# Attention of a two-layer vision block: the engines' loop over 364 window pairs replaced by straight code

## What is computed

```python
qkv = jnp.einsum('bhwc,cd->bhwd', x, w_qkv)
qkv = qkv + jnp.concatenate([q_bias, jnp.zeros_like(q_bias), v_bias])
qkv = jnp.roll(qkv, (-SHIFT, -SHIFT), axis=(1, 2))
...
q = _l2norm(q) * jnp.exp(scale)
k = _l2norm(k)
attn = jnp.einsum('bnhqd,bnhkd->bnhqk', q, k)
...
attn = attn + bias + jnp.asarray(_SHIFT_MASK)
attn = jax.nn.softmax(attn, axis=-1)
out = jnp.einsum('bnhqk,bnhkd->bnhqd', attn, v)
...
return jnp.einsum('bhwc,cd->bhwd', out, w_proj) + b_proj
```

## Time and profile before

| | us |
|---|---|
| median of 3 runs | 10940.03 |
| lowest and highest | 10927.17, 10954.37 |
| the profiled execution, its own time | 10950.05 |
| its span in the trace | 10948.2 |
| busy: GpSimd | 6207.5 (57%) |
| busy: VectorE | 5565.9 (51%) |
| busy: TensorE | 4602.7 (42%) |
| busy: ScalarE | 3954.9 (36%) |

### The profile page before, as it was taken

The page is one execution under the profiler, slowest core; times in us unless marked ns, Lnnn a source line. Parts: engine busy times, 40 slices in busy tenths (PEclk is TensorE's granted clock), DMA queues, the critical chain, the costliest instruction groups (busy, mean ns, idle before and its releaser), DMA issues. The chain is left out here.

```text
span 10948.2 us, 130025 instructions
## 1 busy us (share of the span) xinstructions
PE 4602.7 (42%) x31813; PEld 2736.9 (25%) x31813; DVE 5565.9 (51%) x14498; ACT 3954.9 (36%) x9657; POOL 6207.5 (57%) x6259
## 2 busy tenths in 40 slices
PE   0011777777775998874232222322323323223000
PEld 0011555555553544551111111111101101101000
DVE  9987999999996776551211211212212112112477
ACT  0011877777782554332121211212212212112255
POOL 0000545444451222666777777777777777777675
PEclk9755999999897999876666666666666666666555
DMA  0000111111112222553222222222222222222366
GB/s 21 0 0 36 38 34 37 37 38 37 37 34 85 62 61 75 145 136 60 45 49 44 45 48 44 47 45 46 47 44 47 48 41 49 47 41 49 137 239 242
DMA packets 1325947, 662.48 MB, mean 61 GB/s; under 512 B 1058256, under 2 KB 1239101, under 8 KB 1320765
## 3 DMA queue, kind: packets, MB, share of 16 engines
q1 hardware_dynamic: 1142396, 576.49, 19.3%
q0 software_dynamic: 183104, 80.22, 6.2%
HBM read 344.86 MB, written 313.71 MB: 60 GB/s over the span
## 5 line engine op out<-in xcount | busy, mean ns | idle before, releaser
L1838 POOL DMA_INDIRECT gr_rec<-rec,gr_idx x4096 | 3960.0, 967 | 1248.8 <-issue 1247.9
L1859 PE MATMUL gr_p_h<-gr_tT,gr_w 128*128 128x512 f32 x1568 | 847.2, 695 | 3678.2 <-ACT gr_hT L1893 3646.2
L1978 DVE TENSOR_SCALAR gr_pen<-gr_same 128x64 f32<-128x64 f32 x64 | 13.5, 211 | 3168.1 <-DMA gr_rec<-rec,gr_idx 3168.1
L546 POOL TENSOR_TENSOR at_sq<-at_qk 128x256 f32<-128x256 f32 x392 | 294.2, 750 | 1972.9 <-ACT at_qk L595 1972.3
L1859 PEld LDWEIGHTS gr_p_h<-gr_tT,gr_w 128*128 128x128 f32 x1568 | 347.8, 227 | 4159.1 <-ACT gr_hT L1893 3731.3
L1906 ACT ACTIVATE gr_ee<-gr_dd 128x512 f32<-128x512 f32 x64 | 40.3, 629 | 3595.9 <-DVE gr_dd L1997 3595.9
L1864 PE MATMUL gr_p_y<-gr_hT,gr_w 128*128 128x512 f32 x1568 | 688.9, 592 | 0.0
L1958 DVE STREAM_TRANSPOSE gr_z<-gr_yb 128x2048 f32<-128x2048 f32 x98 | 226.5, 2311 | 893.9 <-ACT gr_yb L1898 863.2
L1893 ACT ACTIVATE gr_hT<-gr_p_h,gr_b 128x512 f32<-128x512 f32 x784 | 517.7, 688 | 189.4 <-PE gr_p_h L1859 186.1
L2146 POOL DMA_INDIRECT cb_a<-scan,cb_idx x392 | 503.0, 1283 | 133.6 <-issue 121.0
L1342 POOL DMA_INDIRECT adst<-co_rec,co_idx x448 | 422.9, 944 | 218.9 <-issue 146.6
(11 more groups left out here) (364 smaller groups left out, 13064.6 us busy)
## 6 DMA issues: line engine op xcount, KB each, us to landing
y<-gr_z SPq DMA_DIRECT2D x392, 256.0 KB, 5.2
cb_y<-y SPq DMA_DIRECT2D x28, 3584.0 KB, 13.1
gr_rec<-rec,gr_idx POOLq DMA_INDIRECT x4096, 2.4
scan<-gr_out SPq DMA_DIRECT2D x64, 768.0 KB
at_xs<-in_x_win SPq DMA_DIRECT2D x56, 448.0 KB, 3.8
x<-at_x SPq DMA_DIRECT2D x56, 448.0 KB, 4.4
ff_x<-x SPq DMA_DIRECT2D x56, 448.0 KB, 3.3
x<-ff_x SPq DMA_DIRECT2D x784, 32.0 KB
```

The costliest lines, as they stand in the source:

```text
L546: nc.gpsimd.tensor_tensor(sq[r][:, :], qk[r][:, :], qk[r][:, :], ALU.mult).then_inc(S["sq"], 1)
L1838: nc.gpsimd.indirect_dma_start(out=rec[s][:, j, :], out_offset=None, in_=rec_dram, in_offset=bass.IndirectOffsetOnAxis(ap=idx[s][:, j:j + ...
L1859: nc.tensor.matmul(p_h[m % 4][:, :], w1[:, P * m:P * (m + 1)], tT[b.k][:, :], start=True, stop=True).then_inc(S["hp"], 1)
```

## The change

The loop instruction of each engine is replaced by a Python loop, so that the 26 bodies are emitted one after another. `i` is then a Python integer, and with it everything that `Step` makes of it: the pair's number `t`, the strip's number, the semaphore targets of all waits, the column offsets in `rp`, `stats` and `score`, the DRAM addresses of the strip's load and store, and the row of `bm` that `last_row` picks (its branch for integers is taken, L314). The instructions on the engines, their order, waits and tiles are the same.

```diff
@@ -405,7 +405,7 @@
 
             for u in range(-4, HALF):
                 emit(Step(eng, u, u, 0, 0, True, False))
-            with eng.Fori(1, STRIPS // 2 - 1) as i:
+            for i in range(1, STRIPS // 2 - 1):
                 for u in range(HALF):
                     emit(Step(eng, u, i * HALF + u, i * 2, i, False, False))
             for u in range(HALF + 3):
```

## The result

| | before | after |
|---|---|---|
| median, us | 10942.22 (4 runs, 10927.17 to 10954.37) | 10831.44 (4 runs, 10825.73 to 10839.16) |
| the profiled execution, us | 10950.05 | 10839.16 |
| its span in the trace, us | 10948.2 | 10837.3 |

The ratio is 0.9900, with an interval of 0.9883 to 0.9917: 111 us less, where 79 were forecast, and 3 us inside the lower end of the stated range (10828). A later measurement of the same kernel gave 10832.14 us and 0.9902 (0.9888 to 0.9916).

What follows compares the result with a forecast made beforehand. VectorE, 91% busy, was taken to bound attention, with its idle time at jumps back. Readings of 78, 81 and 83.5 us for one saving gave 79, the other terms nothing: median 10861 us, range 10828 to 10892.

Steps and rivals of the forecast that it cites:

- case C: Attention: each straight body as good as the best halves seen, 75.69 us; gain 99 us, 10841 us; chance 0.03.
- Part 1: VectorE's taken branch: idle time before L704 goes, 3.25 us for each of 25 edges, 81.2 us; 83.5 by body lengths.
- Part 2: ScalarE's 1.28 us table load at each body's start, uncovered in straight code: 0.4 us lost per body.
- rival B: Gain halved as ScalarE's table load (29 us) or code fetch (44 us) shows in each body: 10895 us; chance 0.08.
- Part 3: TensorE's 25 edges, 88.6 us, and slow clock around them go; costed at nothing, covered by VectorE's own work.
- Part 4: VectorE's register instructions run ahead beside its work and show only at body starts: 0 added, bounds 0 and 20 us.
- Part 5: All five engines stream new code in sequence for 2,000 us: taken as 0, bounds 0 and 44 us.
- The body: Length of a straight attention body of fourteen pairs: 39.09 + 37.46 = 76.55 us, against 79.65 us in the loop.
- The signs: Expected in the trace: L704 idle under 5 us, bodies 76 to 77, attention 75 to 85 sooner, more 8 KB packets.
- D: VectorE's idle time at body starts isn't the jump's; only the branch's 68 ns is saved, 2 us: 10938 us; chance 0.02.
- E: Slower: later loops at new addresses lose held code, 11055 us, or straight code stalls on fetches, 11012 us; chance 0.04 for both.

Runs made afterwards that it cites:

- announced jumps: Kernel before with its loop kept, plus one instruction at the head of each body announcing the jump back: 10888.6 us, ratio 0.9953.
- register numbers: Straight code of the full change, but VectorE holds the body's number in a register and works out wait targets and addresses from it: 10879.5 us, ratio 0.9944.

## Why the prediction was right or wrong

Sign, main mechanism and range were right (10861 forecast, 10828 to 10892, 10831 measured), but the range held by 3 us only. Two terms were mis-sized in opposite directions, and that they partly cancel is luck. The measured 111 us lie nearer to case C (99 us, chance 0.03) than to the forecast's 79, and register work, one of C's two reasons, was the larger of the two errors.

- **Part 1, the jump, 81 to 83.5 us.** Right. The row fell from 81.6 to 0, and the announced jumps split it into 64 us of fetch and 17 us that stay at the bodies' starts, 11 of them register work without any jump. The 3.25 us per jump held with half of the jumps left (3.3 us).
- **Part 2, the table load: 0.4 us per body.** Under-sized. The wait for `rs` rose by 22 us, to 32.0, and leaving out the loads is worth 24 us, 0.9 us per body. That is nearer to the 29 us of rival B than to the 10 us taken.
- **Part 3, TensorE, costed at nothing.** Right for this change, and its reason wrong. "The largest wait of VectorE for TensorE is 1.7 us" was true only because VectorE stood still at the same moments. With TensorE's loop kept, 58 of the 83 us that the two engines are worth together did not come. The cover that I ought to have named was VectorE's own pause, not its work. What TensorE's higher clock (0.91, now 0.95) is worth by itself, no run shows.
- **Part 4, register work: 0, bound 20 us.** This is the term that failed. It costs VectorE 39 us of the stage in the run with register numbers, of which 11 us lie at the bodies' starts and so were in part 1; the pairs of lines above have 34.6 us outside those starts. Its place is the operations with register addresses (L688 to L690, L1593 to L748). I had compared seven epilogue pairs with the loop's, 39.09 with 38.61 and 39.23 us. The same seven pairs, with the same code, take 37.90 us in the kernel after. Before, they held 1.5 us of waiting for `rs` and an odd 0.8 us at L748; after, 1.0 us and nothing. Those 1.3 us hid just the register work. The timeline of one strip of the kernel before (0.58 us from L1593 to L1595, with 0.17 us of work in L1595) would have shown it.
- **Part 5, fetch in sequence.** Right: "issue" rows of VectorE are 5.9 and 1.0 us, all small.
- **The body.** The forecast took 39.09 + 37.46 = 76.55 us for a straight body. In the kernel after its first seven pairs take 38.1 us in the mean and the second seven 37.3, 75.4 together. 25 × 1.1 = 28 us are the whole difference between 79 and the stage's 106.
- **The sum.** By the pairs of lines the stage's gain is 88.9 + 34.6 − 26.7 + 9.3 = 106.1 us: body starts, register addresses, table load, and all others net, among them operations that overlap less with GpSimd's products.
- **The signs.** Bodies of 76 to 77 us, attention 75 to 85 us sooner, and more packets on the queue of 8 KB packets did not come: they are 75.4 us, 106 us, and 191 packets for 189. (With VectorE alone in straight code that queue has only 118; straight ScalarE adds 59 and straight GpSimd 13, so the number stood still by two opposite changes.) The packets of 16 KB fell, from 258 to 203; they fell to the same 203 when only TensorE's code was made straight, so it was TensorE that had read code again at its jumps.
- **Rivals.** D fell with the announced jumps. With it falls, as the price of a jump, the 108 ns that the Trainium skill (Advanced Engine Details and Errata, Control Flow Timing) gives a compare-and-branch: VectorE's branch record is that short (68 ns), the jump is not. B's mechanism exists (the table load), at 22 to 24 us, and the register work more than outweighed it. E didn't happen: 208 ns in the later loops.

## What to carry to other kernels

Look at the first operation of a loop body in the timeline, engine by engine. If it stands behind microseconds of "issue" after each branch, straight code or announced jumps give them back, but in full only if every engine that pauses there is treated, since pauses at the same moment cover each other (25 and 17 us for one engine, 83 for both). Look next at operations whose output or input address contains the loop's number: on a saturated VectorE the three from L688 to L690 cost 0.2 us per strip here, and those from L1593 to L748 0.35 us. And what the pause had hidden (here a table load per body) is best moved out in the same edit: here it took the gain from 111 to 132 us (10939.7 − 10807.7).

## What the runs showed of the hardware that I had not expected

- A jump back costs VectorE 2.6 us and TensorE 3.5 us of waiting for code here, while ScalarE and GpSimd show no such wait in the same loop (branches of 45 and 53 ns); the announcement instruction removes it on both, at 31 to 39 ns each, and with it nearly all instruction packets of the stage.
- Register instructions are not free on an engine that has enough queued work: a VectorE copy with a register address and the operation ahead of it are each some 0.1 us longer, and there are gaps around them. With the body starts it is 39 us over 26 bodies.
- VectorE operations that overlap a GpSimd product can last twice as long (640 for 341 ns at 1997.97), and once three times. Fewer of them are long after the change, which is part of the 9 us net that no other term explains; that it is a change of phase between the two engines is not shown.
